# Transformer decoder block on one core: the products with V of the self-attention in bursts of eight instead of four, with eleven tiles of exponentials instead of eight

## The chip, the cores and the metric

The kernel runs on one core of one Trainium2 chip. The metric is the device time of one execution in microseconds (us). Before the change it is 1962.59 us, the median of three runs (1958.56 to 1962.68).

## The reference, cut to what matters

A decoder block over B = 4 sequences of S = 1024 tokens, D = 256 channels and H = 16 heads of 16 channels: self-attention with latent projections and rotary terms, cross-attention to a context of 154 tokens, and a layer of 8 experts in which each expert picks its 256 tokens; each of the three is followed by a layer norm. The change touches the self-attention:

```
attn = jnp.einsum('bhqd,bhkd->bhqk', query, key) / scale
attn = jax.nn.softmax(attn, axis=-1)
out = jnp.einsum('bhqk,bhkd->bhqd', attn, value)
```

## The kernel before

For each of the 4 sequences there is a self-attention stage, then projections and norms, a cross-attention stage, and again projections and norms. The experts follow at the end, over all sequences.

The operands of the scores are split into bf16 parts, stacked over 96 rows (three more rows, 99 in all, carry minus the row maximum). A self-attention stage works on 8 groups of 2 heads. For each head the scores are computed twice:

- Maximum products (`maximum`, L1442): for one head and one tile of 128 queries, two matmuls of 512 columns fill a pair of PSUM banks. VectorE reduces the pair to minus the row maximum (L1034). There are two pairs, banks 0 to 3, so the products of unit n wait until the reduction of unit n - 2 has ended (`s_smu`). 16 units make a group, 128 a stage.
- Transposed scores ("st", L1492): for one head, one tile of 128 keys and half of the queries, one matmul of 512 columns writes one of the banks 4, 5 and 6. ScalarE takes the exponential of the bank into a tile of the ring `pT` (L881). The product for a bank waits until the exponential before it in that bank has ended (`s_ex`). 32 units make a group, 256 a stage. After the last maximum product of a stage, banks 0 to 3 join the three.
- Products with V ("av", L1524): the tile of `pT` is multiplied in fp32 by 32 columns that hold V and a column of ones. Four of them, one for each head and half of the group, stand side by side in the four column strips of the array and write the four strips of bank 7 (`AV_BANK`). They accumulate over the 8 tiles of keys of the group. Each is issued as two matmul instructions.
- Turns ("turn", L1476, then L889): once a group, GpSimd splits the maxima in four short operations (L703 to L709), TensorE transposes them into one of the score banks, ScalarE copies them out (L889) and three DMAs (L513) put them into the stack.
- Emptying: ScalarE copies bank 7 to `oT` (L872) once a group, after the exponential that is 5 units further than the group's last tile (`EMPTIED`). The first product with V of the next group waits for it (`s_ave`).

All three engines walk through one list, `ORDER_SELF` (or `ORDER_NEXT`, where the first group's maxima were done in the cross-attention stage before), which `schedule` writes out. For every unit st it places half a maximum unit, so that away from the turns the order on TensorE between two bursts is: st, maximum, st, st, maximum, st; and then one burst. `burst_end` gives the last product with V of a burst. A burst is put into the list when its last unit is at most st - `LAG`, with `LAG` = 3. On TensorE a burst waits, before its first product, for the exponential of its last (`made`, from the same `burst_end`). ScalarE waits before the exponential of unit n for the product with V of unit n - `RING_P`, which used the tile before.

In the last group there are no maxima left, and the order is four st, one burst. The cross-attention has groups of 5 units and uses `burst_end` too.

The lists with the unit numbers, as `schedule` writes them before the change (s is st, M a maximum unit, a a product with V, T a turn):

```
... s31 M38 s32 s33 M39 s34 a28 a29 a30 a31 s35 M40 s36 s37 M41 s38 a32 a33 a34 a35 s39 ...
... s50 a44 a45 a46 a47 s51 M48 s52 s53 M49 s54 a48 a49 a50 a51 T2 s55 M50 s56 ...
... s250 a244 a245 a246 a247 s251 s252 s253 s254 a248 a249 a250 a251 s255 a252 a253 a254 a255
```

Of the kernel before, what the change touches and what calls it, by code (L numbers as in the profile page):

```python
# [51 lines left out]
TILES = G * HALVES  # L52
NG = H // G
# [72 lines left out]
ST_SELF, ST_CROSS = NG * HALVES * T * G, NG * (TILES + 1)  # L126
LAG = 3
EMPTIED = 5
RING_P = 8
AV_BANK = 7  # L130


def burst_end(av, st_group):

    return av + min(TILES, st_group - av % st_group) - 1


def schedule(sm_group, st_group, lead, turn):

    order, av, sm = [], 0, 0  # L140
    for k in range((NG + 1) * st_group + lead):
        while sm < NG * sm_group and sm * st_group < (k + 1) * sm_group:
            order.append(("smax", sm))
            sm += 1
        if k >= st_group + turn and (k - turn) % st_group == 0 and (k - turn) // st_group <= NG:
            order.append(("turn", (k - turn) // st_group - 1))
        st = k - st_group - lead
        if st >= 0:
            order.append(("st", st))
        last = burst_end(av, st_group)  # L150
        if last <= st - LAG:
            order += [("av", n) for n in range(av, last + 1)]
            av = last + 1
    return order + [("av", n) for n in range(av, NG * st_group)]
# [51 lines left out]
def decoder_block(nc, a, out):  # L206
    ctx = ExitStack()
    with ctx:  # L208
        def sb(name, shape, dt=F32):
            return ctx.enter_context(nc.sbuf_tensor(name, shape, dt))  # L210
# [48 lines left out]
        maskb = sb("maskb", [P, T, 160], BF16)  # L259
        pT = sb("pT", [P, RING_P, N])  # L260
        full, rest = pT[:, 4:6, :], pT[:, 6:8, :]
# [547 lines left out]
        def _(act):  # L809
# [51 lines left out]
            def attention(b, n0, g0, units, order, banks, scale, kept):  # L861
# [12 lines left out]
                for what, n in order:  # L874
                    if what == "st":
                        act.wait_ge(s_st, b * ST_ALL + n0 + n + 1)
                        if n == 4:
                            act.wait_ge(s_p4, b * PIECES + kept)
                        if n0 + n >= RING_P:
                            act.wait_ge(s_pu, b * ST_ALL + n0 + n - RING_P + 1)  # L880
                        act.activation(pT[:, n % RING_P, :], PS[:, banks[what, n], :], ACT.Exp,  # L881
                                       scale=scale).then_inc(s_ex, 1)
# [474 lines left out]
        def _(pe):  # L1357
# [91 lines left out]
            def attention(b, n0, u0, g0, order, cross):  # L1449
# [15 lines left out]
                for what, n in order:  # L1465
# [47 lines left out]
                    else:  # L1513
                        g, k = divmod(n, per)
                        if k % TILES == 0:
                            made = b * ST_ALL + u0 + burst_end(n, per) + 1
                            (wait_apart if cross and k == TILES else wait)(pe, s_ex, made)
# [4 lines left out]
                        if not cross:  # L1522
                            kc, j = divmod(k, TILES)
                            ins = pe.matmul(av[V32 * j:V32 * (j + 1), :], Vf[:, kc, (g * G + j // HALVES) * VD:(g * G + j // HALVES) * VD + V32], pT[:, n % RING_P, :],  # L1524
                                            start=(kc == 0), stop=(kc == T - 1), tile_position=(0, V32 * j),
                                            skip_group_check=True)
                        elif k < TILES:
                            ins = pe.matmul(av[V32 * k:V32 * (k + 1), :], Vx[:, g * G + k // HALVES, :], pT[:, n % RING_P, :],
                                            start=True, stop=False, tile_position=(0, V32 * k),
# [302 lines left out]
```

## Time and profile before

| | |
|---|---|
| median of three runs | 1962.59 us |
| profiled execution, its own time | 1959.72 us |
| its span, first to last instruction | 1957.9 us |
| TensorE busy | 1668.1 us, 85% |
| VectorE busy | 1134.5 us, 58% |
| ScalarE busy | 891.8 us, 46% |
| GpSimd busy | 429.8 us, 22% |
| mean granted TensorE clock | 0.907 |

The span and the execution's own time differ by 1.8 us, which lie around the span. PE is TensorE's matmuls, PEld its weight loads, DVE VectorE, ACT ScalarE, POOL GpSimd. Matmuls are pipelined, so that each shows its whole length (about 0.38 us for 512 columns in bf16) while the next begins earlier: the distance between two starts is what one costs. Shares over the whole span mix stages with different limits. The four self-attention stages last about 185 us each (from the first st to the last: from 97.7, 476.6, 858.1 and 1239.9 us on), 740 us in all.

### The profile page before, as it was taken

To read this page: it belongs to the slowest core of one execution; us is meant where nothing else is said; L and a number is where in the kernel's file an instruction comes from. 1 tells how busy PE (TensorE), PEld (TensorE's weight loads), DVE (VectorE), ACT (ScalarE), POOL (GpSimd) and SP (SyncE) were. 2 spreads that over 40 slices of the span, in tenths; PEclk is the share of its full clock that TensorE was granted. 3 is DMA by queue.
4 is the path that set the end of the run, shared out by engine and by line. 5 is a ranking of instruction groups with operands and counts; after the bars stand their busy time and mean duration, and the time that the engine had idled before them with its cause. 6 is when DMAs were issued, how large, how long until landed. Compare 5 with 4: busy or idle time off the path is not lost. (4 is left out here: it accounts for less than half of the span.)

```text
span 1957.9 us, 32981 instructions
## 1 busy us (share of the span) xinstructions
PE 1668.1 (85%) x10632; PEld 848.3 (43%) x10632; DVE 1134.5 (58%) x1939; ACT 891.8 (46%) x1585; POOL 429.8 (22%) x547
## 2 busy tenths in 40 slices
PE   6599988798999888989998798999967844999993
PEld 3033334444332445433324354333245433888883
DVE  5577725756777256567763665677435366333424
ACT  2077773342777534347774343577833300111112
POOL 5200004302000052020001611100031001555563
PEclk9599999897999988979998899799988955999997
DMA  6700003622000044220000632200003040335446
GB/s 187 163 2 1 2 25 87 163 48 71 2 2 2 27 127 134 49 59 2 2 2 27 164 98 53 54 2 2 2 21 78 2 150 28 75 77 107 77 89 193
DMA packets 98037, 120.07 MB, mean 61 GB/s; under 512 B 17180, under 2 KB 73500, under 8 KB 97820
## 3 DMA queue, kind: packets, MB, share of 16 engines
q1 hardware_dynamic: 85468, 97.13, 18.1%
q0 software_dynamic: 12416, 20.98, 5.7%
q8 instruction: 86, 1.41, 0.3%
q14 instruction: 67, 0.55, 0.1%
HBM read 80.30 MB, written 40.79 MB: 62 GB/s over the span
## 5 line engine op out<-in xcount | busy, mean ns | idle before, releaser
L881 ACT ACTIVATE pT<-banks 128x512 f32<-128x512 f32 x1184 | 645.2, 596 | 254.8 <-PE banks L1492 150.0
L1034 DVE TENSOR_REDUCE nmf<-banks 128x1 f32<-128x1024 f32 x512 | 606.0, 1220 | 173.5 <-PE banks L1442 171.6
L1492 PE MATMUL banks<-qst,kst 99*128 99x512 bf16 x1024 | 344.0, 388 | 12.1 <-DVE nmf L1034 6.3
L1442 PE MATMUL banks<-kst,qst 96*128 96x512 bf16 x1024 | 327.0, 404 | 31.9 <-DMA kst<-k_parts 21.8
L1524 PE MATMUL banks<-pT,V 128*32 128x512 f32 x2048 | 273.8, 606 | 20.6 <-ACT oT L872 14.0
L1492 PEld LDWEIGHTS banks<-qst,kst 99*128 99x128 bf16 x1024 | 96.0, 97 | 307.2 <-ACT pT L881 185.8
L703 POOL CAST nmp<-nmf 128x16 bf16<-128x16 f32 x64 | 12.7, 198 | 831.4 <-DVE nmf L1034 516.6
L944 ACT ACTIVATE kst<-banks 128x512 f32<-128x512 f32 x64 | 38.2, 597 | 287.0 <-PE banks L1747 278.6
L1442 PEld LDWEIGHTS banks<-kst,qst 96*128 96x128 bf16 x1024 | 98.6, 100 | 146.4 <-DVE nmf L1034 37.3
L1029 DVE TENSOR_REDUCE nmf<-banks 128x4 f32<-128x616 f32 x128 | 99.6, 797 | 86.6 <-PE banks L1436 79.7
L1053 DVE RECIPROCAL rz<-banks 128x16 f32<-128x16 f32 x64 | 16.1, 251 | 204.5 <-PE banks L1552 203.4
L1277 DVE TENSOR_SCALAR kst<-banks,gate 128x256 f32<-128x256 f32 x64 | 28.0, 479 | 169.3 <-issue 164.6
L777 POOL DMA_INDIRECT acc_rows<-kst,tok_s x64 | 103.5, 1617 | 101.6 <-issue 97.7
L889 ACT ACTIVATE nmT<-banks 6x1024 bf16<-6x1024 bf16 x64 | 64.7, 1011 | 128.2 <-PE banks L1476 127.9
L1760 PE MATMUL banks<-qst,kst 128*128 128x256 f32 x512 | 120.8, 390 | 0.0
L1433 PE MATMUL banks<-maskb,identb 128*128 128x308 bf16 x256 | 79.3, 322 | 45.6 <-DVE V L1098 24.7
L1747 PE MATMUL banks<-kst,qst 128*128 128x256 f32 x512 | 117.9, 384 | 0.0
L1760 PEld LDWEIGHTS banks<-qst,kst 128*128 128x128 f32 x512 | 97.6, 194 | 12.9
L1747 PEld LDWEIGHTS banks<-kst,qst 128*128 128x128 f32 x512 | 96.5, 193 | 12.3
L1524 PEld LDWEIGHTS banks<-pT,V 128*32 128x32 f32 x2048 | 41.3, 108 | 132.3 <-ACT pT L881 131.3
L716 POOL TENSOR_TENSOR rstd<-ve,mhalf 128x4 f32<-128x4 f32 x16 | 16.3, 1018 | 331.0 <-DVE ve L1079 331.0
L770 POOL DMA_INDIRECT kst<-x_rows,tok_g x64 | 63.4, 991 | 88.7 <-DVE tok_s L1266 66.6
(176 smaller groups left out, 2016.7 us busy)
## 6 DMA issues: line engine op xcount, KB each, us to landing
qst<-q_parts SPq DMA_DIRECT2D x48, 256.0 KB, 5.2
kst<-k_parts SPq DMA_DIRECT2D x48, 256.0 KB, 3.8
qst<-in_w SPq DMA_DIRECT2D x16, 512.0 KB
q_parts<-kst SPq DMA_DIRECT2D x48, 128.0 KB, 2.5
k_parts<-kst SPq DMA_DIRECT2D x48, 128.0 KB, 3.9
qx_parts<-kst SPq DMA_DIRECT2D x48, 128.0 KB, 3.1
qxs<-qx_parts SPq DMA_DIRECT2D x24, 256.0 KB, 5.0
qst<-qx_parts SPq DMA_DIRECT2D x24, 256.0 KB, 4.9
```

Of the source, the lines that this page charges most:

```text
L770: pool.indirect_dma_start(xg[b][:, j, :], None, x2_rows, bass.IndirectOffsetOnAxis(tok_g[half][:, b, j:j + 1], 0)).then_inc(s_g[b], 16)
L777: pool.indirect_dma_start(acc_rows, bass.IndirectOffsetOnAxis(tok_s[half][:, b, j:j + 1], 0), yg[b][:, j, :], None, compute_op=ALU.add).th ...
L881: act.activation(pT[:, n % RING_P, :], PS[:, banks[what, n], :], ACT.Exp, scale=scale).then_inc(s_ex, 1)
L889: act.activation(nmT[:, m % 2, :], PS[0:3 * G, banks[what, n], :].bitcast(BF16), ACT.Copy).then_inc(s_ne, 1)
L1029: dve.tensor_reduce(nmf[:, m % 2, j, 4 * u:4 * u + 4].rearrange("p (a t) -> p a t", a=2), scores[:, :, 0:2 * SK].rearrange("p a (t k) -> p ...
L1034: dve.tensor_reduce(nmf[:, m % 2, j, t:t + 1], scores.rearrange("p a n -> p (a n)"), AX.X, ALU.max, negate=True).then_inc(s_smu, 1)
L1433: pe.matmul(ps[:, 0:2 * SK], identb[:, :], maskb[:, t0:t0 + 2, 0:SK], start=True, stop=False, skip_group_check=True)
L1442: ins = pe.matmul(pair[:, half, :], qst[0:KQ, h, t * P:(t + 1) * P], kst[0:KQ, h, half * N:(half + 1) * N], start=True, stop=True)
L1492: ins = pe.matmul(ps, kst[0:KM, head, kc * P:(kc + 1) * P], qst[0:KM, head, cols], start=True, stop=True)
L1524: ins = pe.matmul(av[V32 * j:V32 * (j + 1), :], Vf[:, kc, (g * G + j // HALVES) * VD:(g * G + j // HALVES) * VD + V32], pT[:, n % RING_P, ...
L1747: ins = pe.matmul(PS[:, 2 + 2 * k + f // 2, (f % 2) * CAP:(f % 2 + 1) * CAP], we1[half][:, c, f * P:(f + 1) * P], xgT[k][:, c, :], start=( ...
L1760: ins = pe.matmul(PS[:, 6 + k, j * D:(j + 1) * D], hT[k][:, f, j * P:(j + 1) * P], we2[half][:, f, :], start=(f == 0), stop=(f == F // P - 1))
```

## The change

In the self-attention a burst ends at the next multiple of eight units of the group, and no longer at the next multiple of four. The ring has eleven tiles (22 KB in each partition, before 16 KB). The cross-attention, whose group has another size, keeps its bursts and gets the longer ring too.

```
-RING_P = 8
+RING_P = 11
+BURST = 8
 AV_BANK = 7


 def burst_end(av, st_group):

-    return av + min(TILES, st_group - av % st_group) - 1
+    k = av % st_group
+    return av + min(BURST - k % BURST if st_group == ST_SELF // NG else TILES, st_group - k) - 1
```

The list of `schedule` becomes, in the same places:

```
... s31 M38 s32 s33 M39 s34 a24 a25 a26 a27 a28 a29 a30 a31 s35 M40 s36 s37 M41 s38 s39 M42 s40 s41 M43 s42 a32 ... a39 s43 ...
... s50 a40 ... a47 s51 M48 s52 s53 M49 s54 T2 s55 M50 s56 s57 M51 s58 a48 ... a55 s59 ...
... s250 a240 ... a247 s251 s252 s253 s254 s255 a248 ... a255
```

The wait for `made` stands before each product whose unit is a multiple of four; in a burst of eight the first one already waits for the eighth exponential.

## Rows read from the trace of the kernel before

**Rows 1.** The page's second part: granted TensorE clock in 40 slices of the span.
```profile
PEclk9599999897999988979998899799988955999997
```
**Rows 2.** Groups by line, second sequence's stage: busy, mean ns | idle before, releasers.
```profile
L881 ACT ACTIVATE pT<-banks 128x512 f32<-128x512 f32 x256 | 137.7, 596 | 38.9 <-PE banks L1492 36.3
L1034 DVE TENSOR_REDUCE nmf<-banks 128x1 f32<-128x1024 f32 x107 | 126.5, 1220 | 32.2 <-PE banks L1442 32.0
...
L1524 PE MATMUL banks<-pT,V 128*32 128x512 f32 x504 | 67.2, 604 | 4.5 <-ACT oT L872 3.5 <-ACT pT L881 0.6
```
**Rows 3.** Windows: that stage; busy of PE, PEld, DVE, ACT, POOL, then clock.
```profile
476.60:661.50 184.90, 177.32 (x1027) 54.08 (x1025) 125.56 (x107) 146.53 (x270) 7.88 (x29) 0.99 0.01 2
```
**Rows 4.** Timeline of one cycle with maxima: start, length, engine, line.
```profile
523.60 0.39 PE L1492 MATMUL banks<-qst,kst 99*128 99x512 bf16 x1
523.82 0.60 PE L1442 MATMUL banks<-kst,qst 96*128 96x512 bf16 x2
524.02 1.74 ACT L881 ACTIVATE pT<-banks 128x512 f32<-128x512 f32 x3 [0.61 <-PE banks L1492]
...
524.46 1.22 DVE L1034 TENSOR_REDUCE nmf<-banks 128x1 f32<-128x1024 f32 x1 [0.48 <-PE banks L1442]
524.69 0.60 PE L1442 MATMUL banks<-kst,qst 96*128 96x512 bf16 x2
525.13 0.38 PE L1492 MATMUL banks<-qst,kst 99*128 99x512 bf16 x1
...
525.44 0.64 PE L1524 MATMUL banks<-pT,V 128*32 128x512 f32 x4
...
525.60 1.21 DVE L1034 TENSOR_REDUCE nmf<-banks 128x1 f32<-128x1024 f32 x1
525.89 0.61 PE L1524 MATMUL banks<-pT,V 128*32 128x512 f32 x4
526.43 0.39 PE L1492 MATMUL banks<-qst,kst 99*128 99x512 bf16 x1
```
**Rows 5.** Timeline at a stage's start, where maxima follow each other.
```profile
473.34 2.35 DVE L1034 TENSOR_REDUCE nmf<-banks 128x1 f32<-128x1024 f32 x2
...
475.75 0.61 PE L1442 MATMUL banks<-kst,qst 96*128 96x512 bf16 x1
```
**Rows 6.** Timeline around a turn.
```profile
516.56 0.61 PE L1524 MATMUL banks<-pT,V 128*32 128x512 f32 x4
516.99 0.61 PE L1476 MATMUL banks<-identb,nmp 128*6 128x128 bf16 x8
517.53 0.39 PE L1492 MATMUL banks<-qst,kst 99*128 99x512 bf16 x1
517.72 1.01 ACT L889 ACTIVATE nmT<-banks 6x1024 bf16<-6x1024 bf16 x1 [0.81 <-PE banks L1476]
...
518.79 0.39 PE L1492 MATMUL banks<-qst,kst 99*128 99x512 bf16 x1 [0.22 <-ACT nmT L889]
```
**Rows 7.** What ended TensorE's idle time before L1524, whole span: us, times.
```profile
  ACT oT L872: 14.0, 28
```
**Rows 8.** Timeline of the last group, without maxima, in two places.
```profile
636.19 2.06 ACT L881 ACTIVATE pT<-banks 128x512 f32<-128x512 f32 x4 [0.72 <-PE banks L1492]
...
650.28 1.04 PE L1492 MATMUL banks<-qst,kst 99*128 99x512 bf16 x4
651.36 1.07 PE L1524 MATMUL banks<-pT,V 128*32 128x512 f32 x8
652.36 0.39 PE L1492 MATMUL banks<-qst,kst 99*128 99x512 bf16 x1
```
**Rows 9.** Timeline where the maxima of the stage end.
```profile
632.27 0.60 PE L1442 MATMUL banks<-kst,qst 96*128 96x512 bf16 x2
634.45 0.39 PE L1492 MATMUL banks<-qst,kst 99*128 99x512 bf16 x1 [1.58 <-DVE nmf L1034]
```
**Rows 10.** Timeline of two bursts back to back, end of the last cross-attention.
```profile
1543.64 0.64 PE L1528 MATMUL banks<-pT,Vx 128*32 128x512 f32 x4
1544.20 0.63 PE L1534 MATMUL banks<-pT,Vr 26*32 26x512 f32 x4
```

## Prediction

> **What bounds the kernel now.** I began with the page and with the windows of one self-attention stage, since the change touches nothing else. In the stage TensorE is busy 177.3 of 184.9 us at a granted clock of 0.99, ScalarE 146.5 and VectorE 125.6 [rows 3]; the low digits of the clock lie in other stages [rows 1]. TensorE therefore sets the pace, but the groups by line show that the two others follow closely: both wait almost only for TensorE, ScalarE 36 us before the exponentials and VectorE 32 us before the reductions [rows 2]. So the question is how the work of all three falls within one cycle, and I read the timeline [rows 4].
>
> A cycle of four goes from one st to the same place after the next burst: 523.60 to 526.43, 2.83 us. In it 8 bf16 matmuls start about 0.22 us apart. From the last of them to the burst it is 0.31 us, 0.09 more than between two bf16 matmuls. The burst's first four fp32 instructions start together, the second four 0.45 us later, and the next st 0.54 us after that, 0.09 more than the 0.45. A switch into the burst and out of it thus costs 0.18 us [rows 4]. VectorE starts a reduction 0.64 us after its first matmul (523.82 to 524.46), the next 1.14 us after it, each lasts about 1.22 us, and then it idles 0.48 us. ScalarE starts an exponential 0.42 us after its st, then one each 0.49 us (four in 2.06 us, of which the last takes 0.60) [rows 4, 8]. Where TensorE waits for a reduction, its matmul starts 0.06 us after the end: 473.34 + 2.35 = 475.69, then 475.75 [rows 5].
>
> **What the change removes.** Each stage has 64 bursts before and 32 after. Over 4 stages 128 switches go; by 0.18 us they are 23 us. And the group's first product with V, which waited for the emptying of bank 7 28 times, 14.0 us in all [rows 7], comes four units later. If TensorE stayed the bound, that would be the answer. The Trainium skill, page "TensorEngine Tiling (Array Packing)", section "Key Properties", says that a change of tiling mode drains the engine; by that rule alone the sum would be the 23 us gained, and the 0.18 us of rows 4 agree that there is such a price. I don't let it decide, because the longer stretch between bursts meets the other engines.
>
> **A plain block of eight, with maxima.** Let 0 be the first st after a burst. Before, it lasts 2 x 2.83 = 5.66 us. After, the order is st M st st M st, and without a burst again st M st st M st. First reduction: 0.22 + 0.64 = 0.86 to 2.08. Second: 2.00 to 3.21. The third maximum unit needs the pair of the first: it would come at 1.96, but starts at 2.08 + 0.06 = 2.14. The fourth needs the second: free of it at 3.00, it starts at 3.21 + 0.06 = 3.27. Behind each waits the rest of TensorE's queue. Its two matmuls take 0.44, so the last st is at 3.71, the burst at 4.02, and the next st after 3 x 0.45 + 0.54 = 1.90 us, at 5.92. That is 0.26 longer. Before, the burst in the middle gave VectorE that time (it idled 0.48 us in each cycle); now VectorE gets two pairs too quickly and then 1.3 us of nothing. There are 13 such blocks in a stage, counted with the first: 13 x 0.26 = 3.4 us.
>
> **Blocks with a turn.** A turn (6 in blocks with maxima) now lies in the middle of the block. Before: after the second half of the burst 516.56 the turn starts at 516.99 and st at 517.53, so 0.97 instead of 0.54, and the third st after it, due 0.88 later at 518.41, waits until 518.79 for the copy: 5.66 + 0.43 + 0.38 = 6.47 [rows 6]. After: turn at 1.73, copy 0.73 later for 1.01, the waiting st at 3.53 (0.06 behind), then a maximum unit and the last st in 0.65, burst 0.31 later, 1.90: about 6.4 to 6.5. VectorE catches up behind the turn. Nothing gained or lost. From the turn to the next group's first st it is nine units and eight products with V in both orders, so the three DMAs (L513) have the same time. **Blocks with an emptying** (6): before 5.66 + 0.5 = 6.1 [rows 7]; after, no wait, but the copy holds ScalarE 0.49 us, and an st that needs a bank comes some 0.1 late: 5.92 + 0.1 = 6.0. A gain of 0.1 x 6 = 0.6 us. **The block in which the maxima end**: bank 0 may be taken for st only after the last reduction. Before, the st comes at 634.45, 2.18 after the last maximum unit (due at 1.09 in its cycle): 2.83 + 1.09 + 2.18 + 0.31 + 0.45 + 0.54 = 7.40 [rows 9]. After: fourth reduction from 0.86 + 3 x 1.14 = 4.28 to 5.50, st at 5.56, + 0.31 + 1.90 = 7.77. Loss 0.4.
>
> **The last group, without maxima.** Here a burst waits for the exponential of its last tile. Before, that is the first exponential after the last burst: 0.42 + 0.60 + 0.05 = 1.08 after the st (650.28 to 651.36), cycle 2.08 [rows 8], so 4.16 for eight. After, the burst of eight stands behind eight st, and waits for the fifth of their exponentials: 0.42 + 4 x 0.49 + 0.60 + 0.05 = 3.02. The burst takes 1.90, the block 4.92: 0.76 longer. ScalarE has only three exponentials left when the burst starts, and idles through most of it. LAG has remained 3, and the seven banks don't help since the burst stands ahead of the next st in the queue. Three plain blocks lose 2.3 us; the one with the turn, where the copy (1.01 us) lies among the five, some 0.6; the one with the emptying, which already waited for 1.1 us, 0.2. At the end five st and then eight products follow: the burst starts at 3.02 and takes 1.90; before, a cycle of 2.08, then an st, 1.08 to its burst and 0.99 for it: 3.02 + 1.90 against 2.08 + 1.08 + 0.99, a loss of 0.8. Sum 3.9 us.
>
> **Sum.** 3.4 + 0 - 0.6 + 0.4 + 3.9 = 7.1 us a stage; worked through unit by unit in the same way, with the small differences between blocks, I get 7.5. Four stages: 30 us. The tiles themselves cost nothing: the longer ring only lets the exponential of unit n + 11 wait for product n, which is what bursts of eight behind a lag of 3 need, and it never makes an exponential of the cross-attention wait that didn't before.
>
> **The unknown price** is that between the two halves of a burst of eight, since no two bursts of this shape follow each other in the trace. From below it is the 0.43 us from a burst's last half to a turn [rows 6]; from above the 0.56 us between two bursts of different strips (1543.64 to 1544.20) [rows 10]. I take the 0.45 that stands within a burst, which it is nearest to. 32 x 4 such places: -3 us, or +14 us.
>
> So the profiled execution's 1959.7 + 30 = 1990; the median of the three runs is 2.9 above that execution, hence 1991 with both in mind.
>
> **Rivals.**
> (1) Faster. The third and fourth maximum units don't wait, because VectorE is done earlier than I take from the cycle, and TensorE remains the bound there. Then a plain block is 5.92 - 0.46 = 5.46, 0.20 shorter than before: 13 x -0.20, the emptyings -0.6 x 6, the end of the maxima +0.4 and the last group +3.9 as above: -1.9 a stage, 1960 - 8 = 1952. It decides at 0.26 us: a pair of reductions must end that much sooner than 2.35 us. For it speaks that TensorE is the busiest engine; against it that 1.22 us shows no spread to speak of [rows 2], and that the wait on the pair is in the queue's order. Chance 0.06.
> (2) Only one of the two losses. If ScalarE's exponentials were further ahead in the last group than three, its block would stay near 4.1, and the stage lose 7.5 - 3.9 = 3.6: 1974. Chance 0.12.
> (3) A gap in the middle of a burst of eight as between different strips, 0.56: 30 + 14 = 44, 2004. For it speaks that the second four tiles of a burst need weights of their own, and that in no row more than two halves follow each other in the same strips. Chance 0.13.
> (4) The added idle time lets the granted clock fall from 2.4 to 1.2 GHz in the last group. TensorE's stretch of 3.02 + 1.90 would be some 2 us longer a block, 5 blocks a stage, 40 us: 2030. The clock is 0.99 in the stage although it waits 1.6 us in one place [rows 3, 9]. Chance 0.03.
> The forecast itself 0.64, own range 1984 to 1997; 0.02 for what I don't see, below or within the noise.
>
> Range 1974 to 2006. A measurement of this kernel tells about 0.2% (4 us) from no change. Faster 0.06, same 0.02, slower 0.92.
>
> **What would show it.** In the profile after, a plain block from st to st past a burst of eight should be 5.9 us, with two waits on VectorE of about 0.2 and 0.3 us before L1442, and VectorE's reductions in groups of four 1.14 us apart. The row of L1524 should lose its wait for L872 and gain one for L881, about 1.2 us a block in the last group. The four stages should last about 192 us each instead of 185, the rest be unchanged. I am wrong if blocks with maxima are shorter than 5.66 us, or if the halves of a burst start further apart than 0.45 us.

## The result and the profile after

The changed kernel takes 1981.3 us, the median of four runs (1975.5 to 1990.7), against 1960.6 before (four runs, one more than in the table of before). The ratio is 1.0113, 95% interval 1.0069 to 1.0157: slower by about 22 us, and clear of noise. The forecast was 1991, within 1974 to 2006, slower; the median lies 10 us under it and outside the narrower range of 1984 to 1997. The profiled execution happened to be the longest of the four, 1990.7 us; beside the profiled one of before it is 31 us longer, where the sum said 30. So the sum fits the profile, but not entirely for its reasons: with the blocks as they were measured it gives 23 us, and nearly all the rest of the 31 is the granted clock in that one execution. A second measurement of the same kernel (below) gives 26 us, between 21 and 32. Both are taken apart below.

The windows of the changed kernel show the second sequence's stage, from its first st to the start of the last product with V, in the columns of [rows 3]; and two short stretches of it:

```profile
484.30:678.90 194.60, 181.51 (x1034) 56.64 (x1034) 123.75 (x107) 142.67 (x270) 7.69 (x29) 0.97 0.02 4
...
492.00:654.00 162.00, 155.71 (x903) 48.99 (x903) 117.98 (x102) 119.29 (x225) 5.90 (x28) 1.00 0.01 2
661.00:665.00 4.00, 3.80 (x18) 0.79 (x19) 0.00 (x0) 1.62 (x4) 0.00 (x0) 0.57 0.00 0
```

To the same point the stage took 185.6 us before. The granted clock is 1.00 in its long middle and 0.57 in four microseconds near its end, which the second sequence's stage of before did not have (its first sequence's had one, shown below under the falls of the clock).

The groups by line of the same stage:

```profile
L883 ACT ACTIVATE pT<-banks 128x512 f32<-128x512 f32 x256 | 134.4, 607 | 56.0 <-PE banks L1494 54.5
L1036 DVE TENSOR_REDUCE nmf<-banks 128x1 f32<-128x1024 f32 x107 | 124.9, 1219 | 36.8 <-PE banks L1444 36.5
...
L1526 PE MATMUL banks<-pT,V 128*32 128x512 f32 x512 | 63.2, 612 | 8.1 <-ACT pT L883 8.1
...
L1444 PEld LDWEIGHTS banks<-kst,qst 96*128 96x128 bf16 x210 | 18.3, 100 | 24.9 <-DVE nmf L1036 12.4 <-issue 1.9
```

ScalarE idles 56 us and no longer 39, though its work is the same [rows 2]. Before the products with V the wait for the emptying (3.5 us there) is gone and one of 8.1 us for the exponentials stands in its place. The weight loads of the maximum products now wait 12.4 us for VectorE. The profile books this wait at the load, and the matmul starts with it (both at 532.64 below).

The timeline of one plain block of eight, with maxima (two windows, joined):

```profile
530.50 0.39 PE L1494 MATMUL banks<-qst,kst 99*128 99x512 bf16 x1
530.72 0.60 PE L1444 MATMUL banks<-kst,qst 96*128 96x512 bf16 x2
...
531.59 0.60 PE L1444 MATMUL banks<-kst,qst 96*128 96x512 bf16 x2
532.03 0.59 PE L1494 MATMUL banks<-qst,kst 99*128 99x512 bf16 x2
...
531.36 4.62 DVE L1036 TENSOR_REDUCE nmf<-banks 128x1 f32<-128x1024 f32 x4 [1.60 <-PE banks L1444]
...
532.64 0.11 PEld L1444 LDWEIGHTS banks<-kst,qst 96*128 96x128 bf16 x2 [0.32 <-DVE nmf L1036]
532.64 0.60 PE L1444 MATMUL banks<-kst,qst 96*128 96x512 bf16 x2
533.08 0.60 PE L1494 MATMUL banks<-qst,kst 99*128 99x512 bf16 x2
533.77 0.11 PEld L1444 LDWEIGHTS banks<-kst,qst 96*128 96x128 bf16 x2 [0.47 <-DVE nmf L1036]
533.77 0.60 PE L1444 MATMUL banks<-kst,qst 96*128 96x512 bf16 x2
534.21 0.38 PE L1494 MATMUL banks<-qst,kst 99*128 99x512 bf16 x1
534.52 1.93 PE L1526 MATMUL banks<-pT,V 128*32 128x512 f32 x16
536.38 0.39 PE L1494 MATMUL banks<-qst,kst 99*128 99x512 bf16 x1
```

From 530.50 to 536.38 it is 5.88 us, against twice 2.83 to 2.84 before [rows 4]. The third maximum unit starts 2.14 us into the block and the fourth at 3.27, to the hundredth where the reductions' ends put them. VectorE works four reductions in one piece of 4.62 us, after 1.60 us of waiting. The burst of sixteen instructions takes 1.86 us to the next st, not 1.90: its instructions start in four lots of four, the second lot 0.45 us after the first, the third and the fourth 0.43 us after the one before.

The timeline of the last group after, two blocks, the first with the emptying and the second plain (three windows, joined):

```profile
657.68 1.90 PE L1494 MATMUL banks<-qst,kst 99*128 99x512 bf16 x8
...
659.08 0.60 ACT L874 ACTIVATE oT<-banks 128x512 f32<-128x512 f32 x1
659.55 3.07 ACT L883 ACTIVATE pT<-banks 128x512 f32<-128x512 f32 x6
661.20 1.83 PE L1526 MATMUL banks<-pT,V 128*32 128x512 f32 x8 [1.62 <-ACT pT L883]
...
661.93 2.81 PE L1526 MATMUL banks<-pT,V 128*32 128x512 f32 x12
...
664.67 1.07 PE L1494 MATMUL banks<-qst,kst 99*128 99x512 bf16 x4
...
667.74 1.93 PE L1526 MATMUL banks<-pT,V 128*32 128x512 f32 x16 [1.13 <-ACT pT L883]
669.60 1.90 PE L1494 MATMUL banks<-qst,kst 99*128 99x512 bf16 x8
```

The plain block ends with its burst from 667.74 to 669.60 and lasts 4.93 us (the others 4.89), where four units and their burst took 2.08 before [rows 8]: all st come at once, TensorE waits 1.13 us for the exponential of the burst's last tile, and then streams 1.86 us, during which ScalarE runs out of work. In the block with the emptying TensorE waits 1.62 us, and right behind it the burst takes 3.47 us (661.20 to 664.67): its last twelve instructions are spread over 2.81 us, the lots of four 0.85 apart instead of 0.43. The granted clock there is the lower of the two levels, 1.2 GHz.

### The profile page after: what moved, and what is told of

Read it like the earlier page. It is cut to its first block and busy times, and to the rows that moved or that the text cites. A ratio compares the mean times of both kernels' runs of the same rounds, so it can differ in the third digit from the quotient of the medians.

```text
span 1988.8 us, 32966 instructions
## 1 busy us (share of the span) xinstructions
PE 1673.3 (84%) x10632; PEld 851.3 (43%) x10632; DVE 1126.8 (57%) x1939; ACT 875.0 (44%) x1585; POOL 430.0 (22%) x547
## 5 line engine op out<-in xcount | busy, mean ns | idle before, releaser
L883 ACT ACTIVATE pT<-banks 128x512 f32<-128x512 f32 x1184 | 632.2, 606 | 319.4 <-PE banks L1494 218.4
L1036 DVE TENSOR_REDUCE nmf<-banks 128x1 f32<-128x1024 f32 x512 | 599.5, 1219 | 188.8 <-PE banks L1444 180.0
L1444 PE MATMUL banks<-kst,qst 96*128 96x512 bf16 x1024 | 331.0, 408 | 38.3 <-DMA kst<-k_parts 22.0
L1494 PE MATMUL banks<-qst,kst 99*128 99x512 bf16 x1024 | 333.2, 389 | 15.2 <-DVE nmf L1036 6.6
L1526 PE MATMUL banks<-pT,V 128*32 128x512 f32 x2048 | 252.6, 611 | 32.6 <-ACT pT L883 32.6
L1444 PEld LDWEIGHTS banks<-kst,qst 96*128 96x128 bf16 x1024 | 88.8, 101 | 171.5 <-DVE nmf L1036 85.6
L1526 PEld LDWEIGHTS banks<-pT,V 128*32 128x32 f32 x2048 | 54.3, 110 | 165.7 <-ACT pT L883 122.8
```

The costliest lines, as they stand in the source:

```text
L1036: dve.tensor_reduce(nmf[:, m % 2, j, t:t + 1], scores.rearrange("p a n -> p (a n)"), AX.X, ALU.max, negate=True).then_inc(s_smu, 1)
L1444: ins = pe.matmul(pair[:, half, :], qst[0:KQ, h, t * P:(t + 1) * P], kst[0:KQ, h, half * N:(half + 1) * N], start=True, stop=True)
L1494: ins = pe.matmul(ps, kst[0:KM, head, kc * P:(kc + 1) * P], qst[0:KM, head, cols], start=True, stop=True)
```

## The experiments

Where a time is given without a profile line, it is the distance from one st to the eighth st after it in the timeline of the named kernel ("a block"), at the full clock where nothing else is said. A "fall of the clock" is a short stretch at 1.2 GHz in the middle or at the end of a stage. Ratios are to the kernel before, on the same chip.

**The ring alone.** The kernel before with

```
-RING_P = 8
+RING_P = 11
```

> The kernel before with the ring of eleven tiles and bursts of four. Theory (bursts of eight meet waits on VectorE and ScalarE): the ring alone changes nothing, ratio 1.000 within 0.003, a plain block of eight units stays 5.67 us, the wait for the emptying of bank 7 stays 14 us. Rival (the longer ring itself costs, by the new place of the tiles in memory or by looser waits): a part of the 20 to 31 us shows here.

Ratio 1.0003 (0.9988 to 1.0019). Plain blocks 5.67, last group 4.15, and TensorE's wait for the emptying 14.0 us in 28 places as in [rows 7]. The ring and the new places in memory make no difference that the ratio can tell (0.2%).

**Bursts of eight only in groups 0 to 6.**

```
+    long = st_group == ST_SELF // NG and av < (NG - 1) * st_group
+    return av + min(BURST - k % BURST if long else TILES, st_group - k) - 1
```

> Bursts of eight in groups 0 to 6 only, the last group in bursts of four. Theory: plain blocks 5.88 us as in the changed kernel, the blocks of the last group back at 4.15 us and no fall of the clock there; per stage about +2.3 us on before, 9 us in all, about 1970. Rival (the blocks with maxima are harmless and the loss is all in the last group): within 3 us of before.

1968.7 us, ratio 1.0075 (1.0057 to 1.0094). Plain blocks 5.88, blocks with an emptying 6.03 (6.14 before), so the blocks with maxima do cost by themselves. The loss is 15 us where I expected 9: the edit spares less than I wrote. Products with V lag behind st, so two blocks without maxima (5.74 with the turn, 4.89) still end in a burst of eight of group 6. Only the last three and the end are back at 5.22, 4.15 and 4.15 us. By the blocks it is 3.5 us a stage, 14 us in four, which fits the ratio.

**Bursts of eight only in the last group.** The same with `av >= (NG - 1) * st_group`.

> Bursts of eight in the last group only. Theory: plain blocks with maxima 5.67 us, the last group's 4.9 us with a wait of 1.2 us before each burst, and the end 0.9 us later; about +3.8 us a stage, 15 us in all, and up to 6 us more where the clock falls in the burst after the group's emptying: 1976 to 1982. Rival (the loss is that of the blocks with maxima): no more than 4 us on before.

1967.1 us, ratio 1.0074 (1.0051 to 1.0098). Blocks with maxima 5.67 and 6.14 as before, the last three 5.38, 4.89 and 4.89. The clock didn't fall there in any of the four stages, and the two blocks without maxima ahead of these ran on bursts of four at 5.15 and 4.15. On this chip the kernel before took 1953.8 us, so by the ratio it is 14 us longer (10 to 19), just under the 15 to 21 I gave. That closeness is partly luck: the blocks that changed give only 2.4 us a stage, 9.5 us in four, since the 3.8 I had counted held the two blocks that stayed as they were. The clock did fall in two of the four stages elsewhere, where the maxima end (8.05 and 8.16 us instead of 7.43). The two parts together, 0.75% and 0.74%, are the whole within the intervals, and by the blocks too (14 and 9.5 us of 23).

**Each half waits for its own exponentials.** The changed kernel with

```
-                            made = b * ST_ALL + u0 + burst_end(n, per) + 1
+                            made = b * ST_ALL + u0 + (burst_end(n, per) if cross else n + TILES - 1) + 1
```

> The changed kernel, but each half of a burst of eight waits only for its own four exponentials. Theory: in the last group the first half starts with the last st and the second waits for the fifth exponential at 3.02 us, so a block is 3.02 + 0.43 + 0.54 = 4.0 us instead of 4.9; the blocks with maxima keep 5.88 us, since no burst waits for an exponential there. About -4.5 us a stage, with the clock's fall gone -20 to -25 us on the changed kernel's profile, time about 1962 to 1967. Rival (the wait isn't what makes the last group long, but the array's pace in a burst of eight): no change from 1981.

1954.3 us beside 1953.8 for the kernel before, ratio 1.0001 (0.9987 to 1.0015). The timeline of a block of its last group:

```profile
656.05 1.90 PE L1494 MATMUL banks<-qst,kst 99*128 99x512 bf16 x8
657.88 2.27 PE L1526 MATMUL banks<-pT,V 128*32 128x512 f32 x16
660.08 0.39 PE L1494 MATMUL banks<-qst,kst 99*128 99x512 bf16 x1
```

The burst starts 0.31 us behind the last st, stretches over its second wait, and the block is 4.03 us (4.12 in a few), below the 4.15 of before. The blocks with maxima are 5.88 as in the changed kernel. So the loss in the last group was the place of one wait. With it mended, the last group and the end are 1.4 us a stage shorter than before, which pays for most of the 2.1 us that the blocks with maxima cost; the rest, 3 us in four stages, is within the interval.

**Reductions of half the length**, in the kernel before and in the changed one. The first half of the keys is left out of the row maximum; TensorE's work is untouched.

```
-  dve.tensor_reduce(nmf[:, m % 2, j, t:t + 1], scores.rearrange("p a n -> p (a n)"),
+  dve.tensor_reduce(nmf[:, m % 2, j, t:t + 1], scores[:, 1, :],
...
```

> The kernel before, with the reduction taking only the second half of the keys, which leaves the first half out of the row maximum; TensorE's work is the same. It is the base for the next run. Both theories: VectorE wasn't what TensorE waited for away from the stage's start, so a plain block of eight units stays 5.67 us, and the stage gains only at its start and where the maxima end, 1 to 3 us.

> The changed kernel with the same halved reduction (first half of the keys left out of the row maximum). Theory (third and fourth maximum unit wait for VectorE): with reductions of about 0.65 us both waits go, and TensorE's pace is left: 5.46 us before for a plain block, 0.43 a half instead of 0.45 makes it 5.42; if the exponentials bound the st instead, 5.5. Blocks of the last group stay 4.9. Rival (the block is 5.88 because of something in the burst of eight): it stays 5.88.

Bursts of four: ratio 0.9979 (0.9966 to 0.9993), plain block 5.67, unchanged; the block where the maxima end 6.63 instead of 7.43. Bursts of eight: ratio 1.0005 (0.9991 to 1.0019), plain block 5.54, against 5.88 with whole reductions. Its timeline:

```profile
510.59 0.60 PE L1494 MATMUL banks<-qst,kst 99*128 99x512 bf16 x2
510.79 0.69 DVE L1036 TENSOR_REDUCE nmf<-banks 128x1 f32<-128x512 f32 x1 [0.17 <-PE banks L1444]
511.03 0.59 PE L1444 MATMUL banks<-kst,qst 96*128 96x512 bf16 x2
511.46 0.70 PE L1494 MATMUL banks<-qst,kst 99*128 99x512 bf16 x2
511.66 0.69 DVE L1036 TENSOR_REDUCE nmf<-banks 128x1 f32<-128x512 f32 x1 [0.17 <-PE banks L1444]
512.00 0.60 PE L1444 MATMUL banks<-kst,qst 96*128 96x512 bf16 x2
```

With VectorE out of the way, no maximum unit waits for it (it idles before each reduction). The two st at 511.46 cover 0.70 us instead of 0.59: the second waits 0.11 for its bank, that is for ScalarE, and that is the 0.11 between the 5.54 and the 5.42 of TensorE's pace alone. This is the condition of rival 1 made true by force. The saving of the switches then shows, 5.67 to 5.54 in a plain block, while the whole is 5.4 us longer than with bursts of four and the same reductions (1959.5 against 1954.1): the last group keeps its 4.89, and the blocks with an emptying stay at 6.03.

**The maxima further apart.** In each block of the changed kernel that has maxima and no turn the order st M st st M st st M st st M st becomes

```
wanted = "s M s s M s s s M s s M".split()
```

> The changed kernel with the maxima further apart within a plain block of eight: st M st st M st st st M st st M instead of st M st st M st st M st st M st. No work is added or taken. Theory: the third unit comes at 2.16 us and no longer waits, the fourth still waits until 3.27 but has nothing behind it except the burst: 3.27 + 0.22 + 0.31 + 1.86 = 5.66 instead of 5.88 us; also the block where the maxima end gets shorter by some 0.2 to 0.6. About 13 blocks a stage, 3 us, 12 us in all: about 1969. Rival (the order within a block doesn't matter since the cost is in the burst): 1981.

1979.5 us, ratio 1.0117 (1.0094 to 1.014): nothing gained on the changed kernel, and my 5.66 us for the plain block was wrong; it is 5.81. (By the blocks it is 1 us a stage shorter, which the ratios can't tell.) The timeline says why:

```profile
513.57 1.08 PE L1509 MATMUL banks<-qst,kst 99*128 99x512 bf16 x3
514.49 0.60 PE L1459 MATMUL banks<-kst,qst 96*128 96x512 bf16 x2
514.92 0.71 PE L1509 MATMUL banks<-qst,kst 99*128 99x512 bf16 x2
515.47 0.60 PE L1459 MATMUL banks<-kst,qst 96*128 96x512 bf16 x2
516.00 1.92 PE L1541 MATMUL banks<-pT,V 128*32 128x512 f32 x16
```

Three st in a row should cover 2 x 0.22 + 0.38 = 0.82 us and cover 1.08: one waits 0.26 for the exponential three units back, in the bank it wants, and one of the next two waits 0.11. In place of the wait on VectorE stands one on ScalarE, and in the block with the emptying, where ScalarE has one thing more to do, it makes 6.30 of 6.03. Against that the block where the maxima end fell from 7.71 to 5.81: the last st in it now stands ahead of the last maximum unit in the list, so it doesn't take bank 0 and needn't wait for the last reduction. That gain I had put at 0.2 to 0.6.

**Bank 7 emptied one exponential earlier**, in the kernel before, in the self-attention:

```
+                        emptied = 4 if per == ST_SELF // NG else EMPTIED
+                        if n >= emptied and (n - emptied) % per == per - 1:
+                            empty(n - emptied)
```

> The kernel before, with bank 7 emptied one exponential earlier in the self-attention (after unit n + 4 and not n + 5 of the group's last). Nothing else changed. The 14 us that the first product of a group waited for the emptying were the only other gain of the change. Theory: the copy starts 0.49 us earlier and the wait of 0.4 to 0.5 us goes in 28 places, blocks of 6.14 us become 5.7: -11 to -13 us, about 1948, ratio 0.994. Rival (the wait only moves to an st whose bank is freed later by the exponentials behind the copy): 0 to -3 us.

1943.8 us, ratio 0.9931 (0.9913 to 0.9949).

```profile
500.09 0.60 ACT L881 ACTIVATE pT<-banks 128x512 f32<-128x512 f32 x1 [0.61 <-PE banks L1493]
...
500.59 0.59 ACT L872 ACTIVATE oT<-banks 128x512 f32<-128x512 f32 x1
...
501.19 0.38 PE L1493 MATMUL banks<-qst,kst 99*128 99x512 bf16 x1
501.50 1.07 PE L1525 MATMUL banks<-pT,V 128*32 128x512 f32 x8
```

The copy begins 0.92 us into the cycle, and the burst starts 0.31 us behind its st, with no wait. Blocks with an emptying are 5.67, like the plain ones, and of the 14.0 us in 28 places that TensorE waited for the copy 2.5 us in 4 places are left. What the bursts of eight won back by moving the next group's first product four units on (0.11 us a block, since ScalarE then delayed an st) the earlier copy wins whole (0.47), without any of their losses.

**The changed kernel again.**

> The changed kernel once more. Its profiled execution (1990.7 us) was the slowest of four, and it had two things in three of the four stages that I had not put into the sum: the first block of eight at the low clock (7.5 us) and a fall of the clock in the burst after the last group's emptying (7.0 instead of 5.4 us). Theory: these come and go between executions, the other blocks are the same to 0.01 us; an execution without the second has 5.38 there and is some 5 us shorter. Rival (they belong to the kernel): 7.0 us in three stages again.

1987.2 us, ratio 1.0134 (1.0105 to 1.0163), so 26 us longer than before; the profiled execution 1985.5, 5 us under the first. Two stages have 5.38 in the block with the last emptying, two have 6.85 and 6.99. The first full block of a stage is 6.78, 7.17, 6.55 and 7.53 (7.72, 7.54, 7.48 and 7.49 in the first profile). Every plain block in between is 5.88 or 5.89. So these two vary from stage to stage and from run to run, as the theory says. A third one does too: the block in which the maxima end, 7.71 in most stages, is 9.24 in the first stage of the first profile and 8.87 in the third stage of this one (with 5.95 behind it instead of 5.74). All others repeat, but for the rest of a fall that reaches into the next block (4.93, 5.07).

**Three combinations.** Bursts of four where there are maxima, in the last group bursts of eight with a wait for each half, and the earlier copy:

> Bursts of four where there are maxima, bursts of eight with a wait for each half in the last group, and bank 7 emptied one exponential earlier. Theory: plain blocks 5.67, emptying blocks 5.67, last group 4.03 instead of 4.15: 182.5 us a stage less some 0.5, about 3 us in all under the kernel that only empties earlier, ratio 0.992 to before. Rival (bursts of eight are no gain even there): the same as that kernel, 0.993.

1943.0 us, ratio 0.9921 (0.9905 to 0.9938). Blocks 5.67, in the last group 4.52 with the emptying (4.73 with the earlier copy alone), 4.03 and 4.03.

The kernel before with the earlier copy, and the last maximum unit of a stage behind the st that follows it:

```
+END = ORDER_SELF.index(("smax", SM_SELF - 1))
...
+ORDER_SELF[END:END + 2] = ORDER_SELF[END + 1], ORDER_SELF[END]
```

> The kernel before, bank 7 emptied one exponential earlier, and the last maximum unit of a stage put behind the st that follows it, so that this st needn't take bank 0 and wait for the last reduction. Theory: the block where the maxima end falls from 7.43 to 6.1 or less, since a burst now lies under the last reduction: 1.3 us a stage, 5 us in all under the kernel that only empties earlier: ratio 0.990. Rival (the wait only moves to the next st, all of it): 7.4 stays.

1939.7 us, ratio 0.9905 (0.9888 to 0.9921). The block where the maxima end is 6.11 instead of 7.43.

All three together:

> All three of these: bursts of eight in the last group with a wait for each half, earlier emptying, last maximum behind its st. Theory: the gains add, some 8 us under the kernel that only empties earlier, ratio 0.989, about 1935 to 1940 us.

1936.5 us, ratio 0.9887 (0.9865 to 0.9908). It is the fastest, 1.1% under the kernel before. The step from one combination to the next is within the intervals of the ratios; the blocks, which repeat to 0.01 us at the full clock, carry the order between them. Against the earlier copy alone 8 us were expected; by the blocks it is 7.6, by the two ratios 9 (the two kernels ran on different chips).

## Why the prediction was right, step by step

**What bounds the kernel.** Right. TensorE sets the pace only as long as both others get their work evenly; in the profile after they idle more (ScalarE 56 instead of 39 us) while TensorE waits more. The four stages last 191 us each from the first st to the last, where the forecast said about 192.

**A plain block with maxima.** The mechanism was right and shown: both waits lie where the working put them (2.14 and 3.27 us), and with reductions of half the length they go and the block falls under the 5.67 of before. The size was 0.26 us and is 0.21. The term that was off is the unknown price between the halves of a burst: 0.43 us where I took 0.45, and the same inside the second half, so the lower bound held. It makes 0.04 a block.

**Blocks with a turn, an emptying, the end of the maxima.** Forecast 0, -0.1 and +0.4; measured 0 (6.41 or 6.47 against 6.41 or 6.50), -0.11 (6.03 against 6.14) and +0.28 (7.71 against 7.43).

**The last group.** Forecast 0.76 for a plain block, 0.6 with the turn, 0.2 with the emptying where the clock holds, 0.8 at the end. Measured 0.74, 0.59 (5.74 against 5.15), 0.16 (5.38 against 5.22), 0.74 (4.37 against 3.63 from unit 251's st to the last product). That it is the wait for the last tile, and not the array's pace, is shown by splitting it: 4.89 becomes 4.03.

**The sum.** With the measured blocks at full clock: 12 x 0.21 - 6 x 0.11 + 0.28 + 3 x 0.74 + 0.59 + 0.16 + 0.74 = 5.85 us a stage, 23 us in four, where I had 7.5 and 30. Of the difference of 1.6 a stage, 0.9 is in the plain blocks (of which 0.26 for the first, which no profile of this kernel shows at full clock), 0.1 each in the end of the maxima and the emptyings, 0.2 in the last group, and 0.4 is what working unit by unit had added to the terms shown. This agrees with the two ratios: 22 us (14 to 31) and 26 us (21 to 32). The sum was thus some 7 us too high, and its mechanism right.

**The 31 us of the profiled pair** have the rest from the granted clock; outside the stages the changed kernel is 0.8 us shorter. In three of four stages the burst behind the last emptying ran at 1.2 GHz, 1.6 us each, 5 us. The first full block, at the low clock for longer, was 7.5 to 7.7 us instead of 6.0 to 7.6, together 3.6 us more. This needn't be the change's: with bursts of four and the longer ring alone these blocks are 7.85, 7.77, 6.54 and 6.51. Rival 4, to which I gave 0.03, was thus partly there, with an eighth of the price I named. My reason against it was read from one stage: the clock is 0.99 although TensorE waits 1.6 us. In the first stage of the same profile it had fallen right behind that wait (lines below). That I hit 30 in the profile is in part this coincidence.

**The rivals.** Rival 1 (faster) fell. With its condition made true (the halved reductions) the change is still 5.4 us slower and not 8 faster: the plain block is 5.54 and not 5.46, and an emptying's block falls by 0.11 and not by 0.6. Rival 2 (only one of the two losses) fell: both losses are there, and each part alone costs 0.7%. Rival 3 (a gap within the burst) fell: 0.43 us.

**The falls of the clock.** They aren't peculiar to the burst behind the last emptying, nor to the changed kernel. The first stage of the kernel before, and the end of a stage of the kernel with the maxima further apart (timeline, and windows in the columns of [rows 3]):

```profile
256.91 0.39 PE L1492 MATMUL banks<-qst,kst 99*128 99x512 bf16 x1 [1.58 <-DVE nmf L1034]
257.00:261.00 4.00, 4.00 (x17) 0.79 (x20) 0.00 (x0) 2.06 (x5) 0.82 (x4) 0.57 0.00 0
...
668.48 3.57 PE L1541 MATMUL banks<-pT,V 128*32 128x512 f32 x13 [1.78 <-ACT pT L898]
668.50:672.50 4.00, 3.59 (x16) 0.59 (x16) 0.00 (x0) 0.29 (x1) 0.00 (x0) 0.57 0.78 287
```

The 14 profiles (both kernels and all experiments) have 56 self-attention stages and 21 such falls. Each began between 0.2 us before and 1.0 us after the end of a wait of TensorE of 1.58 to 1.78 us; none began at the waits of 1.0 to 1.3 us.

| the wait | stages that have it | falls | cost of one |
|---|---|---|---|
| for the last reduction, where the maxima end (1.58 or 1.66 us) | 36 | 12 | 1.4 to 1.7 us |
| before the burst behind the last emptying (1.62 us) | 20 | 5, all in the changed kernel | 1.6 to 1.7 us |
| before a stage's last burst (1.78 us) | 20 | 4: half reductions with bursts of eight 1, respaced maxima 3 | 0.8 to 1.3 us |

In the 20 stages in which the first of these waits is 0.79 us or less, or gone (half reductions, respaced maxima, the last maximum behind its st), the clock never fell there, and in the 36 whose last group has bursts of four or a wait for each half it never fell in the last group. So in these profiles no fall came without such a wait, but a stage can have them and keep its clock. What decides in which it falls stays open; the changed kernel adds two such waits to each stage. A longer lag with a longer ring, the other way to have the exponentials ready, wasn't tried.

## What to carry to other kernels

A longer burst on the engine that bounds saves its switches (0.18 us each by the rows of before; where the waits that it brings were taken away, a block of eight units became 0.12 to 0.13 shorter), but it also bundles what the other engines get: check, within one cycle, when each buffer that they fill or free is wanted, not how busy they are on average. With two pairs of banks between them, VectorE, which had idled 0.48 us in each 2.83, became the bound as soon as four of its pieces came in a row. And put a wait where the first use is, not ahead of the whole burst; a wait of half a microsecond at a hand-over may need only the other engine's copy one place earlier in its list, which was worth 0.7% here, more than any burst of eight that was tried.

## What the runs showed of the hardware

Bursts of fp32 matmuls in the four column strips join without a gap: the second lot of four instructions starts 0.45 us after the first, the third and fourth 0.43 us after the one before.

The granted clock fell to 1.2 GHz in stages of the changed kernel in which TensorE had waited no longer than 1.66 us at a time before the fall. In the burst behind the last emptying TensorE was busy 3.80 of the 4.00 us around the fall, with 0.57 granted, the lots of four were 0.85 us apart, and the burst took 1.6 us longer. Each of the 21 falls in the middle or at the end of a stage came at a wait of 1.58 to 1.78 us.
